# Maximum pass of an attention kernel: items of 64 queries of two heads in place of 128 queries of one head

## The chip, the cores and the metric

The kernel runs on one core of one Trainium2 chip. The metric is the device time of one execution in microseconds. A core has TensorE (matmuls; in the rows PE, its weight loads PEld), VectorE (DVE), ScalarE (ACT), GpSimd (POOL) and SyncE (SP), which issues most of the DMAs. Each works through its own queue in order and waits on semaphores.

## The reference

One transformer layer in float32, batch 4, sequence 1024, width 128:

```python
Q, K, V = (proj(W_Q), proj(W_K), proj(W_V))          # 16 heads of 8
Q = _apply_rope(Q, cos, sin)
K = _apply_rope(K, cos, sin)
scores = jnp.einsum('bhsd,bhtd->bhst', Q, K) / jnp.sqrt(jnp.float32(D_K))
scores = jnp.where(causal[None, None], scores, -jnp.inf)
attn = jax.nn.softmax(scores, axis=-1)
out = jnp.einsum('bhst,bhtd->bhsd', attn, V)
...
x = _layernorm(x + attention(x) @ W_O.T)
x = _layernorm(x + experts(x))    # 8 experts of 128-512-128 with gelu, top 2 by a softmax gate
```

## The kernel before

The program has three stages. Up to some 46 us it projects Q, K and V, applies the rotation and splits Q and K into three bf16 parts each, which go out to DRAM as stacks and come back as operands of 56 rows a head pair. Then comes attention, interleaved with the output projection, the layer norm, the gate and the routing of the batch before. From some 590 us on the experts run over 72 gathered tiles, and the second norm ends it.

Attention is worked off in 16 units, one for each batch (4) and group of four heads (4). In a unit the four heads sit in two halves of the partitions (parity `par`: rows 0 to 63 and 64 to 127) and two slots. A unit has two passes.

- The maximum pass ("A" items, `pass_a_items`) computes scores with the queries on the partitions of PSUM and the keys along the row, and reduces them to the maximum of each query. An item is one bank of the three-bank ring: 128 queries of one head (or of both slots, where at most 256 keys are needed) by up to 512 keys. 40 items make a unit. Where the item holds the diagonal, two mask products go first (L703 over the last 128 keys, L705 over the last 64): a half identity `half_sb` times `mask_sb` puts -1e30 where a key lies behind the query. Then L708 adds the scores: 64 rows of the array, 128 columns, so form 64*128. VectorE reads the bank with one `tensor_reduce` (L1157) into `mx`.
- The exponential pass has 12 steps. Each computes scores with the keys on the partitions ("QK", L734, two halves of the partitions into two banks, once for each slot), ScalarE takes the exponential (L867), GpSimd blanks the diagonal (L1408), and "PV" (L754, four heads in four column strips of 32, fp32) accumulates the output and the sum of the weights.

The maxima get into the second pass as three more rows of the operand: GpSimd splits `mx` into three bf16 parts (`SPLIT`, L1379 to L1385), TensorE turns them (`MT`, L716), VectorE copies the 48 rows into `mparts` (L1164), and SyncE writes them into `qst` (`MROWS`, L571). The outputs are turned by `OT` (L763) and scaled.

The order is written out by `schedule()`: while unit u goes through its exponential steps, the A items of unit u+1 are dealt out over these steps, in proportion to the steps' columns (`a_quota`). Each step stands as QK of slot 0, half of the items, QK of slot 1, the other items, PV of the step before. In the eight-bank PSUM three banks are the ring, four take the scores of the second pass and one the output. TensorE may fill a ring bank once VectorE has read what stood in it three entries earlier:

```python
if r is not None and r >= RING:
    pe.wait_ge(ring_read, at(r - RING + 1, RING_BATCH))
```

Unit 0 has its maximum pass ahead of everything. The middle batches are a hardware loop of two turns. The maximum pass of the kernel before, on TensorE:

```python
mm(view[:, :, n - P:n], half_sb[rows, 0, :], mask_sb[rows, 0, 0:k, :], ...)
mm(view[:, :, n - P // 2:n], half_sb[rows, 1, :], mask_sb[rows, 1, 0:k, P // 2:P], ...)
for m, slot_ in enumerate(slots):
    last = mm(ring[:, bank, m * n:(m + 1) * n], qst[rows, ...], kst[rows, v % NG, slot_, t0:t0 + n], ...)
```

Of the kernel before, what the change touches and what calls it, by code (L numbers as in the profile page):

```python
# [21 lines left out]
BF16 = mybir.dt.bfloat16  # L22
# [4 lines left out]
P = 128  # L27
B, S, D = 4, 1024, 128
# [10 lines left out]
MROW = 32  # L39

# [24 lines left out]
def pass_a_items():  # L65

    items = []
    for sb in range(BT):
        whole, rest = divmod((sb + 1) * P, CH)
        parts = [(CH * i, CH) for i in range(whole)] + ([(CH * whole, rest)] if rest else [])  # L70
        for t0, n in parts:
            masked = t0 + n == (sb + 1) * P
            if 2 * n <= CH:
                items += [(par, sb, t0, n, (0, 1), masked) for par in (0, 1)]
            else:
                items += [(par, sb, t0, n, (slot,), masked) for slot in (0, 1) for par in (0, 1)]
    return items
# [17 lines left out]
HALF_ROWS = GH * 3 * BT // 2  # L95

A_HALF = sum(1 for it in A_ITEMS if it[1] < CH // P)
# [174 lines left out]
def build(nc, xT, x, w, wg, bg, w1, w2,  # L272
          cs, ident, halves, maskA, before, tile128, tokens, tiles, first_row, out):
    ctx = ExitStack()
    with ctx:
        def sb(name, shape, dt=F32):
            return ctx.enter_context(nc.sbuf_tensor(name, shape, dt))

        def sem(name):
            return ctx.enter_context(nc.semaphore(name))  # L280
# [19 lines left out]
        half_f = sb("half_f", [P, 2, P])  # L300
        half_sb = sb("half_sb", [P, 2, P], BF16)
        mask_f = sb("mask_f", [P, 2, P])
        mask_sb = sb("mask_sb", [P, 2, 2, P], BF16)
# [47 lines left out]
        mx = sb("mx", [P, 2, GH, BT])  # L351
        mx2 = sb("mx2", [P, 2, GH, BT // 2])
        mrem = sb("mrem", [P, 2, GH, BT])
        zero = sb("zero", [P, GH, BT])

        msp_all = sb("msp", [P, 5 * HALF_ROWS], BF16)
        msp = msp_all[:, 0:4 * HALF_ROWS].rearrange("p (u c a j s n) -> p u c a j s n", u=2, c=2, a=2, j=3, s=2)
# [73 lines left out]
        mask_turns = sem("mask_turns")  # L431
        dve = sem("dve")
# [37 lines left out]
        def _(sp):  # L470
# [20 lines left out]
            sp.dma_start(half_f[:, :, :], halves).then_inc(loads, 16)  # L491
            sp.dma_start(mask_f[:, :, :], maskA).then_inc(loads, 16)
# [55 lines left out]
            def visit(e, r, at):  # L548
# [17 lines left out]
                elif e[0] == "MROWS":  # L566
# [82 lines left out]
        def _(pe):  # L649
# [34 lines left out]
            def visit(e, r, at):  # L684
# [7 lines left out]
                if kind == "A":  # L692
# [3 lines left out]
                    par, sb_, t0, n, slots, is_masked = A_ITEMS[i]  # L696
                    rows = slice(64 * par, 64 * par + 64)
                    k = len(slots)
                    if is_masked:
# [218 lines left out]
        def _(ve):  # L918
# [11 lines left out]
            for c in range(NCH):  # L930
# [10 lines left out]
                if c >= 2:  # L941
# [7 lines left out]
            v.tensor_copy(half_sb[:, :, :], half_f[:, :, :]).then_inc(masks_ready, 1)  # L949
            v.tensor_copy(mask_sb[:, :, :, :], mask_f[:, :, :].unsqueeze(2).broadcast_to([P, 2, 2, P])  # L950
                          ).then_inc(masks_ready, 1)
# [190 lines left out]
            def visit(e, r, at):  # L1142
# [8 lines left out]
                if kind == "A":  # L1151
                    unit, i = e[1:]
                    par, sb_, t0, n, slots, is_masked = A_ITEMS[i]
                    hs = slice(2 * slots[0] + par, 2 * slots[-1] + par + 1, 2)
                    dst = mx[:, unit % 2, hs, sb_] if t0 == 0 else mx2[:, unit % 2, hs, sb_ - BT // 2]
                    src = ring[:, bank, 0:len(slots) * n].rearrange("p (k n) -> p k n", k=len(slots))
                    read(v.tensor_reduce(dst, src, AX.X, ALU.max, negate=True))  # L1157
                    if i == NA - 1:

                        ve.wait_ge(ring_read, at(r + 1, RING_BATCH))  # L1160
                        v.tensor_tensor(mx[:, unit % 2, :, BT // 2:BT], mx[:, unit % 2, :, BT // 2:BT],
                                        mx2[:, unit % 2, :, :], ALU.min).then_inc(mx_ready, 1)
# [158 lines left out]
        def _(pool):  # L1321
# [32 lines left out]
            def visit(e, r, at):  # L1354
# [11 lines left out]
                elif e[0] == "SPLIT":  # L1366
# [9 lines left out]
                    none = by_parity(zero[:, :, :])  # L1376
                    part = [msp[:, unit % 2, c, :, j, :, :] for j in range(3)]
# [136 lines left out]
```

## Time and profile before

| | us |
|---|---|
| median of 3 runs | 820.85 |
| lowest and highest | 820.37, 832.62 |
| profiled execution | 823.58 |
| its span, first to last instruction | 821.8 |
| of it up to the first A item | 46.6 |
| attention, 46.6 to 590 | 543.4 |
| experts and output | 231.8 |

The profile is of one execution. Its page lists busy time by engine and groups of instructions by line; the trace behind it can be asked for stretches of time, waits and the chain of work that ended last. A matmul's end is modelled, and matmuls overlap in the pipeline of the array: the start of the next one says more than the length of one.

### The profile page before, as it was taken

The numbers are of one execution on the slowest core, as the hardware profiler recorded it, in microseconds if no ns is written. First come the engines' busy times: TensorE is split into PE (matmuls) and PEld (weight loads), VectorE is DVE, ScalarE is ACT, GpSimd is POOL, SyncE is SP. The second block draws the span as 40 slices with busy tenths as digits, with TensorE's granted clock in tenths as the row PEclk, the third lists the DMA queues.
The fourth block names the chain that finished last, engine by engine and source line by source line (L and its number), as shares of the span: only waits on it lengthen the run. The fifth ranks groups of instructions, "written<-read, shape, count | busy, mean of one in ns | idle before, by whom it ended". The sixth has DMA issues, their size and how long they took to land.

```text
span 821.8 us, 18980 instructions
## 1 busy us (share of the span) xinstructions
PE 683.3 (83%) x5560; PEld 362.6 (44%) x5561; DVE 584.6 (71%) x1467; ACT 443.5 (54%) x840; POOL 320.7 (39%) x577
## 2 busy tenths in 40 slices
PE   7987999999898868989889998988789857899830
PEld 3432333334343222434323333332278857798830
DVE  7886888888979867798988888896436712222266
ACT  2532676666455554556557655556647524466524
POOL 5961223322213265221328512226614555344551
PEclk9975999999879988998989998899989968899985
DMA  8893255011010120101012011000186745687923
GB/s 274 267 343 125 72 132 162 8 46 48 1 48 6 49 74 22 48 1 48 7 47 80 25 38 46 1 3 22 34 211 200 209 122 147 174 225 210 300 85 114
DMA packets 67352, 83.70 MB, mean 102 GB/s; under 512 B 9266, under 2 KB 46776, under 8 KB 67264
## 3 DMA queue, kind: packets, MB, share of 16 engines
q1 hardware_dynamic: 62912, 74.04, 30.5%
q0 software_dynamic: 4352, 8.53, 3.0%
q8 instruction: 49, 0.80, 0.4%
q14 instruction: 39, 0.32, 0.1%
HBM read 55.77 MB, written 26.90 MB: 101 GB/s over the span
## 4 chain that ended last, share of the span: by engine, by line
PE 50%; DVE 22%; issue 9%; ACT 5%; DMA 4%; SPq 4%; another core or an unknown queue 3%; POOL 2%; DVEq 0%; ACTq 0%; POOLq 0%
PE banks L754 14%; DVE mx L1157 14%; PE banks L708 9%; PE banks L823 6%; PE banks L734 5%; PE banks L812 5%; PE banks L703 2%; PE banks L763 2%; ACT region L867 2%; PE banks L655 2%; DMA region<-pairs 1%; ACT x_sb L910 1%; PE banks L832 1%; SPq L597 1%
## 5 line engine op out<-in xcount | busy, mean ns | idle before, releaser
L1157 DVE TENSOR_REDUCE mx<-banks 128x1 f32<-128x512 f32 (+3 forms) x640 | 366.0, 630 | 46.9 <-PE banks L708 41.5
L867 ACT ACTIVATE region<-banks 128x1024 f32<-128x1024 f32 (+3 forms) x256 | 201.3, 840 | 169.4 <-PE banks L734 159.7
L708 PE MATMUL banks<-region 64*128 64x512 bf16 (+3 forms) x768 | 196.0, 352 | 17.2 <-DVE mx L1157 15.1
L734 PE MATMUL banks<-region 64*128 64x512 bf16 (+3 forms) x768 | 141.6, 347 | 20.7 <-ACT region L867 11.4
L754 PE MATMUL banks<-region 128*32 128x512 f32 (+3 forms) x1024 | 123.1, 555 | 0.9 <-POOL region L1408 0.8
L867 ACT ACTIVATE cs_sb<-banks 128x1024 f32<-128x1024 f32 (+2 forms) x128 | 91.2, 759 | 42.4 <-PE banks L734 41.8
L1418 POOL DMA_INDIRECT results<-region,dest x72 | 71.7, 996 | 105.1 <-DVE region L1285 71.9
L703 PE MATMUL banks<-mask_sb,half_sb 64*128 64x128 bf16 (+1 forms) x384 | 84.7, 252 | 22.6 <-DVE mx L1157 17.3
L1279 DVE TENSOR_TENSOR region<-banks,w1e 128x128 f32<-128x128 f32 x72 | 21.0, 291 | 110.8 <-PE banks L812 66.3
L823 PE MATMUL banks<-region,w1e 128*128 128x128 f32 x576 | 83.2, 291 | 19.3 <-ACT region L893 13.9
L1408 POOL TENSOR_SCALAR_AFFINE_SELECT region<-region 128x256 f32<-128x256 f32 x160 | 64.2, 410 | 87.7 <-ACT region L867 85.1
L734 PEld LDWEIGHTS banks<-region 64*128 64x128 bf16 x768 | 42.4, 95 | 122.9 <-issue 47.3
L1408 POOL TENSOR_SCALAR_AFFINE_SELECT cs_sb<-cs_sb 128x256 f32<-128x256 f32 x96 | 38.6, 412 | 143.4 <-ACT cs_sb L867 142.6
L708 PEld LDWEIGHTS banks<-region 64*128 64x128 bf16 x768 | 65.2, 100 | 56.0 <-DVE mx L1157 42.9
L812 PE MATMUL banks<-w_sb,region 128*128 x576 | 83.3, 290 | 3.9 <-issue 1.8
L823 PEld LDWEIGHTS banks<-region,w1e 128*128 128x128 f32 x576 | 75.9, 205 | 21.4 <-ACT region L893 15.6
L901 ACT ACTIVATE region<-banks,w1e 128x128 f32<-128x128 f32 x288 | 82.9, 379 | 0.5 <-PE banks L823 0.5
L812 PEld LDWEIGHTS banks<-w_sb,region 128*128 128x128 f32 x576 | 74.3, 200 | 8.1 <-issue 6.7
L1394 POOL DMA_INDIRECT pairs<-xT_sb,slot x64 | 63.0, 985 | 36.9 <-issue 21.8
L705 PE MATMUL banks<-mask_sb,half_sb 64*128 64x64 bf16 (+1 forms) x384 | 71.3, 209 | 0.0
L893 ACT COPY region<-banks 128x128 f32<-128x128 f32 x72 | 19.2, 267 | 93.1 <-PE banks L832 67.5
L703 PEld LDWEIGHTS banks<-mask_sb,half_sb 64*128 64x128 bf16 x384 | 35.2, 97 | 61.9 <-DVE mx L1157 46.4
(177 smaller groups left out, 687.8 us busy)
## 6 DMA issues: line engine op xcount, KB each, us to landing
w1e<-in_w SPq DMA_DIRECT2D x72, 322.0 KB
region<-stack_q SPq DMA_DIRECT2D x64, 112.0 KB
region<-stack_k SPq DMA_DIRECT2D x32, 224.0 KB
region<-pairs SPq DMA_DIRECT2D x72, 66.0 KB
region<-results SPq DMA_DIRECT2D x8, 512.0 KB, 4.9
stack_q<-x_sb SPq DMA_DIRECT2D x8, 384.0 KB, 3.6
stack_k<-x_sb SPq DMA_DIRECT2D x8, 384.0 KB, 4.5
stack_q<-x_sb SPq DMA_DIRECT2D x8, 256.0 KB, 3.9
```

The lines of the kernel that those rows point to most:

```text
L703: mm(view[:, :, n - P:n], half_sb[rows, 0, :], mask_sb[rows, 0, 0:k, :], start=True, stop=False, skip_group_check=True)
L705: mm(view[:, :, n - P // 2:n], half_sb[rows, 1, :], mask_sb[rows, 1, 0:k, P // 2:P], start=False, stop=False, skip_group_check=True)
L708: last = mm(ring[:, bank, m * n:(m + 1) * n], qst[rows, v % NG, sb_ // 4, slot_, sb_ % 4 * P:(sb_ % 4 + 1) * P], kst[rows, v % NG, slot_, ...
L734: last = mm(score[:, slot_, par, 0:n], kst[rows, u % NG, slot_, j * P:(j + 1) * P], qst[rows, u % NG, c, slot_, s0 - c * CH:s0 - c * CH + ...
L754: last = mm(pv[32 * h:32 * h + 32, s0 - c * CH:s0 - c * CH + n], vx[:, u % NG, j, h, :], probs[(2 * e[1] + slot_) % 6][:, par, 0:n], start ...
L812: last = mm(down[k % 2], hg[:, k % 2, hc * P:(hc + 1) * P], w2_sb[:, bass.ds(e, 1), hc, :].rearrange("p a n -> p (a n)"), start=(hc == 0), ...
L823: last = mm(hidden[k % 2][:, hc * P:(hc + 1) * P], w1e[:, k, hc * P:(hc + 1) * P], xgT[:, k % 2, :], start=(hc == 0), stop=(hc == HC - 1), ...
L867: nc.scalar.activation(probs[i % 6][:, :, 0:n], score[:, i % 2, :, 0:n], ACT.Exp, scale=SCALE).then_inc(exp_done, 1)
L901: nc.scalar.activation(hg[:, k % 2, cols], hidden[k % 2][:, cols], ACT.Gelu_apprx_tanh, bias=w1e[:, k, HID + hc:HID + hc + 1]).then_inc(ge ...
L1157: read(v.tensor_reduce(dst, src, AX.X, ALU.max, negate=True))
L1408: pp.affine_select(out=block_, in_=block_, compare_op=ALU.is_ge, fill=0.0, base=0, pattern=[[0, 2], [1, P]], channel_multiplier=-1).then_i ...
L1418: pp.indirect_dma_start(out=results, out_offset=bass.IndirectOffsetOnAxis(ap=dest[:, k, :], axis=0), in_=ys[:, k, :], in_offset=None, boun ...
```

## The change

An A item becomes 64 queries of two heads, one in each half of the partitions: the head of rows 0 to 63 writes partitions 0 to 63 of the bank, that of rows 64 to 127 the other 64. The queries are cut into 16 pieces of 64, and an item reaches to the end of its piece's keys, (piece + 1) * 64 in place of (sb + 1) * 128. Again 40 items make a unit, 24 with a mask, with 17,408 columns for VectorE in place of 18,432. The mask is one product of 64 rows by 128 columns over the last 64 keys (two identities side by side) in place of two. Each slot of an item has two matmuls with a tile position, 64 rows by 64 columns each. An item without a mask increments a semaphore of its own. `mx`, the split, `mparts` and the DMAs follow: the maxima are `[slot, piece]` with the head pair along the partitions.

The diff, cut to what computes:

```diff
@@ pass_a_items
-    for sb in range(BT):
-        whole, rest = divmod((sb + 1) * P, CH)
+    for piece in range(S // QP):
+        whole, rest = divmod((piece + 1) * QP, CH)
         parts = [(CH * i, CH) for i in range(whole)] + ([(CH * whole, rest)] if rest else [])
         for t0, n in parts:
-            masked = t0 + n == (sb + 1) * P
+            masked = t0 + n == (piece + 1) * QP
             if 2 * n <= CH:
-                items += [(par, sb, t0, n, (0, 1), masked) for par in (0, 1)]
+                items.append((piece, t0, n, (0, 1), masked))
             else:
-                items += [(par, sb, t0, n, (slot,), masked) for slot in (0, 1) for par in (0, 1)]
+                items += [(piece, t0, n, (slot,), masked) for slot in (0, 1)]
...
-HALF_ROWS = GH * 3 * BT // 2
+HALF_ROWS = 3 * PIECES
...
@@ SyncE, MROWS
                     for par in (0, 1):
                         sp.dma_start(qst[64 * par + MROW:64 * par + MROW + 3, v % NG, c, :, :],
-                                     mparts[par * 3 * BT:(par + 1) * 3 * BT, v % 2, c, :]
+                                     mparts[:, v % 2, c, QP * par:QP * (par + 1)]
                                      ).then_inc(mrows[c][v % 2], 16)
@@ TensorE, A
                     if is_masked:
                         view = ring[:, bank, 0:k * n].rearrange("p (k n) -> p k n", k=k)
-                        mm(view[:, :, n - P:n], half_sb[rows, 0, :], mask_sb[rows, 0, 0:k, :], start=True, stop=False,
+                        mm(view[:, :, n - QP:n], half_sb[0:QP, :], mask_sb[0:QP, 0:k, :], start=True, stop=False,
                            skip_group_check=True)
-                        mm(view[:, :, n - P // 2:n], half_sb[rows, 1, :], mask_sb[rows, 1, 0:k, P // 2:P],
-                           start=False, stop=False, skip_group_check=True)
+                    else:
+                        pe.sem_inc(item_turns, 1)
                     for m, slot_ in enumerate(slots):
-                        last = mm(ring[:, bank, m * n:(m + 1) * n], qst[rows, v % NG, sb_ // 4, slot_, sb_ % 4 * P:(sb_ % 4 + 1) * P],
-                                  kst[rows, v % NG, slot_, t0:t0 + n], start=(m == 0 and not is_masked),
-                                  stop=(m == k - 1), skip_group_check=True)
+                        for rows in heads:
+                            last = mm(ring[rows, bank, m * n:(m + 1) * n],
+                                      qst[rows, v % NG, piece * QP // CH, slot_, at_:at_ + QP],
+                                      kst[rows, v % NG, slot_, t0:t0 + n], start=(m == 0 and not is_masked),
+                                      stop=(m == k - 1), tile_position=(rows.start, rows.start), skip_group_check=True)
                     last.then_inc(ring_full, 1)
@@ VectorE, A
-                    hs = slice(2 * slots[0] + par, 2 * slots[-1] + par + 1, 2)
-                    dst = mx[:, unit % 2, hs, sb_] if t0 == 0 else mx2[:, unit % 2, hs, sb_ - BT // 2]
+                    mine = slice(slots[0], slots[-1] + 1)
+                    dst = mx[:, unit % 2, mine, piece] if t0 == 0 else mx2[:, unit % 2, mine, piece - PIECES // 2]
@@ GpSimd, SPLIT
-                    cols = slice(c * BT // 2, (c + 1) * BT // 2)
-                    by_parity = lambda a: a[:, :, cols].rearrange("p (s a) n -> p a s n", a=2)
-                    neg, rest = by_parity(mx[:, unit % 2, :, :]), by_parity(mrem[:, unit % 2, :, :])
+                    cols = slice(c * PIECES // 2, (c + 1) * PIECES // 2)
+                    neg, rest = mx[:, unit % 2, :, cols], mrem[:, unit % 2, :, cols]
```

Two places of TensorE's queue, as they stand in the program. In the changed kernel L707 is the mask product, L713 the scores, L740 QK, L760 PV (before: L703 and L705, L708, L734, L754). In a row the shape is the output's, so `128x384` is 384 keys for 128 columns of the array, `64x384` for 64.

TensorE, unit 0, third step of the exponential pass, with masked items of unit 1; before:

```order
L703 MATMUL banks<-mask_sb,half_sb 128x128 [waits ring_read]
L705 MATMUL banks<-mask_sb,half_sb 128x64
L708 MATMUL banks<-region 128x384
L734 MATMUL banks<-region 128x256 [waits exp_done]
L734 MATMUL banks<-region 128x256
L703 MATMUL banks<-mask_sb,half_sb 128x128 [waits ring_read]
L705 MATMUL banks<-mask_sb,half_sb 128x64
L708 MATMUL banks<-region 128x384
L703 MATMUL banks<-mask_sb,half_sb 128x128 [waits ring_read]
L705 MATMUL banks<-mask_sb,half_sb 128x64
L708 MATMUL banks<-region 128x384
L754 MATMUL banks<-region 32x512 [waits masked,vx_ready,v_read]
```

And the same step now:

```order
L707 MATMUL banks<-mask_sb,half_sb 128x64 [waits ring_read]
L713 MATMUL banks<-region 64x320 x2
L740 MATMUL banks<-region 128x256 [waits exp_done]
L740 MATMUL banks<-region 128x256
L707 MATMUL banks<-mask_sb,half_sb 128x64 [waits ring_read]
L713 MATMUL banks<-region 64x320 x2
L707 MATMUL banks<-mask_sb,half_sb 128x64 [waits ring_read]
L713 MATMUL banks<-region 64x384 x2
L760 MATMUL banks<-region 32x512 [waits masked,vx_ready,v_read]
```

Before, all rows but the last have 128 columns of the array; now the scores have 64, between masks and QK that have 128, so the number changes five times ahead of L760 where it didn't change at all.

TensorE, unit 0, a later step, with items that have no mask; before:

```order
L734 MATMUL banks<-region 128x512 [waits exp_done]
L734 MATMUL banks<-region 128x512
L703 MATMUL banks<-mask_sb,half_sb 128x128 [waits ring_read]
L705 MATMUL banks<-mask_sb,half_sb 128x64
L708 MATMUL banks<-region 128x512
L708 MATMUL banks<-region 128x512 [waits ring_read]
L734 MATMUL banks<-region 128x512 [waits exp_done]
L734 MATMUL banks<-region 128x512
L708 MATMUL banks<-region 128x512 [waits ring_read] x2
L754 MATMUL banks<-region 32x128 [waits masked]
```

And now:

```order
L740 MATMUL banks<-region 128x512 [waits exp_done]
L740 MATMUL banks<-region 128x512
L707 MATMUL banks<-mask_sb,half_sb 128x64 [waits ring_read]
L713 MATMUL banks<-region 64x512 x2
L713 MATMUL banks<-region 64x512 [waits ring_read]
L713 MATMUL banks<-region 64x512
L740 MATMUL banks<-region 128x512 [waits exp_done]
L740 MATMUL banks<-region 128x512
L713 MATMUL banks<-region 64x512 [waits ring_read]
L713 MATMUL banks<-region 64x512
L707 MATMUL banks<-mask_sb,half_sb 128x128 [waits ring_read]
L713 MATMUL banks<-region 64x64 x4
```

Each L713 of 512 keys has a partner for the other head behind the same wait, and the last item of the step is now a short masked one of 64 keys. Around the QK pair in the middle the number of columns changes from 64 to 128 and back.

## Rows read from the trace of the kernel before

**Rows 1.** The page: span, and busy time of each engine.

```profile
span 821.8 us, 18980 instructions
PE 683.3 (83%) x5560; PEld 362.6 (44%) x5561; DVE 584.6 (71%) x1467; ACT 443.5 (54%) x840; POOL 320.7 (39%) x577
```

**Rows 2.** Windows by stage: length; busy us PE, PEld, DVE, ACT, POOL; clock; DMA share, GB/s.

```profile
46.60:73.50 26.90, 20.48 (x97) 7.44 (x97) 22.45 (x42) 5.24 (x7) 12.59 (x14) 0.57 0.85 288
...
85.24:196.20 110.96, 103.02 (x1002) 39.22 (x1003) 97.52 (x189) 75.56 (x105) 33.65 (x100) 1.00 0.27 77
196.20:569.00 372.80, 326.88 (x2812) 131.25 (x2808) 316.78 (x753) 210.93 (x286) 125.61 (x300) 0.92 0.11 33
...
590.00:821.80 231.80, 165.76 (x1312) 156.37 (x1308) 94.56 (x406) 110.93 (x394) 100.15 (x98) 0.86 0.63 177
```

**Rows 3.** Windows of two neighbouring units, same columns.

```profile
112.97:140.71 27.74, 25.66 (x250) 9.68 (x250) 24.35 (x48) 18.91 (x27) 8.41 (x25) 1.00 0.69 187
140.71:168.44 27.73, 25.66 (x250) 9.67 (x250) 24.34 (x48) 18.90 (x27) 8.41 (x25) 1.00 0.11 35
```

**Rows 4.** Chain of work, 140.70 to 168.44 us, then (second row) 300 to 420 us.

```profile
by line: PE banks L754 29.3%; DVE mx L1157 22.2%; PE banks L708 16.0%; PE banks L734 10.2%; issue 7.8%; ACT region L867 6.0%; PE banks L763 4.3%; PE banks L703 2.5%; PE banks L716 1.5%; DVE attn L1172 1.0%; DVE rden L1170 1.0%; PE banks L70
...
140.71 3.08 DVE mx L1157 x5
...
by line: DVE mx L1157 20.3%; PE banks L754 17.6%; PE banks L708 13.2%; issue 12.4%; PE banks L734 7.5%; another core or an unknown queue 5.8%; PE banks L703 3.5%; PE banks L763 2.5%; PE banks L792 1.6%; PE banks L770 1.5%; PE banks L705 1.0
```

**Rows 5.** Timeline of TensorE, 91.5 to 94.6 us: start, duration, form rows*columns.

```profile
91.59 0.28 PE L703 MATMUL banks<-mask_sb,half_sb 64*128 64x256 bf16 x1 [0.19 <-DVE mx L1157]
91.71 0.22 PE L705 MATMUL banks<-mask_sb,half_sb 64*128 64x128 bf16 x1
91.77 0.38 PE L708 MATMUL banks<-region 64*128 64x256 bf16 x2
92.07 1.07 PE L754 MATMUL banks<-cs_sb,region 128*32 128x512 f32 x8
93.07 0.66 PE L763 MATMUL banks<-id_sb,ot 128*128 128x128 f32 x4
93.66 0.39 PE L734 MATMUL banks<-region 64*128 64x512 bf16 x2
93.89 0.38 PE L708 MATMUL banks<-region 64*128 64x512 bf16 x2
94.10 0.38 PE L734 MATMUL banks<-region 64*128 64x512 bf16 x2
94.40 0.39 PE L708 MATMUL banks<-region 64*128 64x512 bf16 x1
```

**Rows 6.** Groups by shape: busy us, mean ns of one.

```profile
L1157 DVE TENSOR_REDUCE mx<-banks 128x1 f32<-128x512 f32 x384 | 243.6, 683 | 24.9 <-PE banks L708 22.0 <-issue 0.6
...
L708 PEld LDWEIGHTS banks<-region 64*128 64x128 bf16 x768 | 65.2, 100 | 56.0 <-DVE mx L1157 42.9 <-DVE attn L1172 5.0 <-DVE y L1222 1.8
L1157 DVE TENSOR_REDUCE mx<-banks 128x1 f32<-128x384 f32 x128 | 63.8, 550 | 10.2 <-PE banks L708 8.6 <-issue 0.7
```

**Rows 7.** Who waited for whom, 140.7 to 168.44 us: us, times, longest.

```profile
DVE mx L1157 <- PE banks L708: 3.3, 10, 0.6
...
PEld banks L708 <- DVE mx L1157: 1.9, 5, 0.6
...
PEld banks L703 <- DVE mx L1157: 1.6, 4, 0.5
```

**Rows 8.** L731 on TensorE's sequencer: ns min/median/max.

```profile
L731 PEldq EVENT_SEMAPHORE  x15: 51/51/51, 82.1 to 574.5; - x15
```

**Rows 9.** Chain before the first QK; who waited for the DMA of L571 (us, times).

```profile
66.90 6.60 DMA region<-mparts
...
  PE banks L734: 3.9, 1
```

**Rows 10.** L1379 on GpSimd, by shape.

```profile
L1379 POOL TENSOR_TENSOR msp<-mx,zero 128x16 bf16<-128x16 f32 x32 | 7.1, 222 | 80.2 <-DVE mx L1157 62.4 <-DVE mx L1161 17.8
```

More of the change, by code:

```diff
@@ L39 @@
 MROW = 32
+QP = 64
+PIECES = S // QP
 Q_PLACES = ((0, (0, 3, 6)), (1, (1, 2)), (2, (5,)))
@@ L94 @@
 C_LAST = [max(k for k, st in enumerate(B_STEPS) if st[0] == c) for c in range(2)]
-HALF_ROWS = GH * 3 * BT // 2
-A_HALF = sum(1 for it in A_ITEMS if it[1] < CH // P)
+HALF_ROWS = 3 * PIECES
+A_HALF = sum(1 for it in A_ITEMS if it[0] < PIECES // 2)
 def diagonal(k):
@@ L299, in build @@
         idb_sb = sb("idb_sb", [P, P], BF16)
[L300 to L303, printed above, removed]
+        half_f = sb("half_f", [P, P])
+        half_sb = sb("half_sb", [P, P], BF16)
+        mask_f = sb("mask_f", [P, QP])
+        mask_sb = sb("mask_sb", [P, 2, QP], BF16)
         fill = sb("fill", [P, 2, S], BF16)
@@ L350, in build @@
         rden = sb("rden", [P, 2, 4 * GH])
[L351 to L354, printed above, removed]
+        mx = sb("mx", [P, 2, 2, PIECES])
+        mx2 = sb("mx2", [P, 2, 2, PIECES // 2])
+        mrem = sb("mrem", [P, 2, 2, PIECES])
+        zero = sb("zero", [P, 2, PIECES])
         msp_all = sb("msp", [P, 5 * HALF_ROWS], BF16)
-        msp = msp_all[:, 0:4 * HALF_ROWS].rearrange("p (u c a j s n) -> p u c a j s n", u=2, c=2, a=2, j=3, s=2)
+        msp = msp_all[:, 0:4 * HALF_ROWS].rearrange("p (u c j s n) -> p u c j s n", u=2, c=2, j=3, s=2)
         mparts = sb("mparts", [HALF_ROWS, 2, 2, P], BF16)
@@ L431, in build @@
         mask_turns = sem("mask_turns")
+        item_turns = sem("item_turns")
         dve = sem("dve")
@@ L490, in _ @@
             sp.dma_start(id_sb[:, :], ident).then_inc(loads, 16)
-            sp.dma_start(half_f[:, :, :], halves).then_inc(loads, 16)
-            sp.dma_start(mask_f[:, :, :], maskA).then_inc(loads, 16)
+            sp.dma_start(half_f[:, :], halves).then_inc(loads, 16)
+            sp.dma_start(mask_f[:, :], maskA).then_inc(loads, 16)
             sp.dma_start(wg_sb[:, :], wg).then_inc(loads, 16)
@@ L1160, in visit @@
                         ve.wait_ge(ring_read, at(r + 1, RING_BATCH))
-                        v.tensor_tensor(mx[:, unit % 2, :, BT // 2:BT], mx[:, unit % 2, :, BT // 2:BT],
+                        upper = slice(PIECES // 2, PIECES)
+                        v.tensor_tensor(mx[:, unit % 2, :, upper], mx[:, unit % 2, :, upper],
                                         mx2[:, unit % 2, :, :], ALU.min).then_inc(mx_ready, 1)
@@ L1372, in visit @@
                         pool.wait_ge(mx_ready, at(unit + 1, NG))
-                    cols = slice(c * BT // 2, (c + 1) * BT // 2)
-                    by_parity = lambda a: a[:, :, cols].rearrange("p (s a) n -> p a s n", a=2)
-                    neg, rest = by_parity(mx[:, unit % 2, :, :]), by_parity(mrem[:, unit % 2, :, :])
-                    none = by_parity(zero[:, :, :])
-                    part = [msp[:, unit % 2, c, :, j, :, :] for j in range(3)]
+                    cols = slice(c * PIECES // 2, (c + 1) * PIECES // 2)
+                    neg, rest = mx[:, unit % 2, :, cols], mrem[:, unit % 2, :, cols]
+                    none = zero[:, :, cols]
+                    part = [msp[:, unit % 2, c, j, :, :] for j in range(3)]
                     done = 8 * unit + 4 * c
@@ L1484 @@
     q, k = np.arange(P)[:, None], np.arange(P)[None, :]
-    row = np.arange(P)[:, None, None] % 64 + 64 * np.arange(2)[None, :, None]
-    col = np.arange(P)[None, None, :]
-    halves = np.where(col == row, np.float32(1.0), np.float32(0.0))
+    row = np.arange(P)[:, None] % QP
+    col = np.arange(QP)[None, :]
+    halves = np.tile(np.where(col == row, np.float32(1.0), np.float32(0.0)), (1, 2))
     mask_a = np.where(col > row, np.float32(-1e30), np.float32(0.0))
```

12 lines of the change are left out of this document (6 added, 6 removed).

## The prediction

> **What bounds the kernel now.** I read the page first, then the windows by stage, then one unit of the attention stage in full. The page gives a span of 821.8 us with TensorE busy 83% and VectorE 71% [rows 1]; these are means over unlike stages, so they settle nothing. The profiled execution took 823.58 us, 2.73 us above the median of the runs (820.85); I work against 823.58 and take 2.7 off at the end. The change touches the maximum pass alone, which lives between 46.6 and 569 us; what stands behind 590 us (231.8 us of experts and output) stays [rows 2]. In the four units from 85.24 to 196.20 us nothing else is interleaved and the clock is 1.00: 27.74 us a unit. The eleven units whose maxima are taken after that have the routing work of an earlier batch beside them: 372.8 us for what is 11 to 12 units, some 31.5 us each, at a mean clock of 0.92 [rows 2].
>
> One unit is so regular that two neighbours agree to 0.01 us: VectorE 24.35 us busy, TensorE 25.66 of 27.74 [rows 3]. Both engines look near full, so the chain decides: of such a unit it spends 22.2% on the maxima of L1157 and more than 60% on TensorE lines (L754 29.3%, L708 16.0%, L734 10.2%, L763 4.3%, L703 2.5%); in a later batch it is 20.3% against some 48%, with 12.4% "issue" [rows 4]. The reader should see an engine pair that takes turns: VectorE rules in runs of consecutive items (five in 3.08 us), TensorE everywhere else.
>
> How full TensorE is by columns: a column takes 1/2.4 ns at the full clock, an fp32 column two. A unit's maximum pass streams 18,432 columns of scores (7.68 us) and 6,144 of masks (2.56), QK 4,608 per slot in pairs (3.84), PV 4,608 x 4 (7.68), the transposes 0.96: 22.7 us. Laying the unit's 250 matmuls [rows 3] side by side by start and columns, 20.6 us are covered; 2.1 us fall together, because matmuls on the two halves of the partitions run at once: two 512-column ones stand in 0.39 us where one alone takes 0.39 too [rows 5].
>
> **The price of another tile shape.** The form names rows*columns of the array. Within 64*128 a matmul follows its predecessor when its columns are through: 256 columns 0.107 us, L703 to L705 0.12; 512 columns 0.213 us, L708 to L734 0.21. Where the shape changes there is more. L708 starts at 91.77 with 2 x 256 columns (0.213), so it is through at 91.98, and L754 (128*32) starts at 92.07: 0.09. From L763 (128*128) to L734 four fp32 transposes need 0.43, and 0.59 pass: at most 0.16. From L754 (128*32) to L763 (128*128), where the number of rows stays and only the columns change, 1.00 us pass for 0.85 of columns: at most 0.15 [rows 5]. I take 0.10 us a change, the clean end of 0.09 to 0.16.
> The Trainium skill, "TensorEngine Tiling (Array Packing)", Key Properties, says that changing the tiling mode, not just the tile, drains the engine, and its list of modes has 64x64 and 64x128 as separate ones. The rows agree for the shapes that occur; the pair 64*128 and 64*64 occurs in none of them.
>
> **The change, part by part.**
> *VectorE.* Still 40 items a unit, but 17,408 columns for 18,432. The maxima cost 683 ns at 512 columns and 550 at 384: 1.04 ns a column [rows 6]. So 1,024 x 1.04 = 1.06 us less a unit, 17 us in all, of which only what lies on the chain counts: 0.2 of it, 0.2 us a unit, about 3.5 us.
> *TensorE, columns.* Scores: 17,408 columns, each streamed for two heads on different quarters of the array, 7.25 us if the two run together. Masks: 24 products of 64 columns a slot, 2,048 columns, 0.85 us for 2.56. Sum with the rest 20.6 us. That is what was covered before: the 2.1 us saved are the 2.1 us that used to fall together, since an item of 64*64 can't share time with a QK of 64*128 if a change lies between.
> *TensorE, shapes.* This is the cost. Mask products stay 64*128 (64 rows, 128 columns), the scores become 64*64, QK stays 64*128. Counting through the order of a batch gives 116 changes before and 324 after: 208 more, 52 a unit (mask to scores 24, scores to the next mask 9, scores to QK 11, QK to unmasked scores 8). 52 x 0.10 = 5.2 us a unit. In unit 0, whose pass runs alone, some 46 more.
> *What hides it.* TensorE's waits. A unit of 27.74 us holds 20.6 of columns, 28 changes (2.8) and about 0.9 of small gaps, so 3.4 us of waits. They are for VectorE above all: the loads of L708 and L703 alone stand 1.9 and 1.6 us behind L1157 (loads run ahead, so not all of this is idle array); VectorE in turn waits 3.3 us for L708 [rows 7]. Afterwards columns, 80 changes and small gaps make 29.5 us: even with no wait left the unit is 1.8 us longer. With all waits kept it is 5.2 longer. The waits sit in the runs that VectorE rules, and there the changes are free; I take a third hidden: 3.5 us a unit, for four units 13.9. In the later units, 31.5 us long with 5 us and more of such waits, I take half: 2.6 us, for eleven units 28.6. Unit 0, where the chain is mostly L1157: a third of 4.6, 1.5.
> *Semaphores on TensorE.* Each of 16 unmasked items a unit increments item_turns. Such an instruction takes 51 ns in the sequencer [rows 8]; between nothing and 16 x 0.051 = 0.8 us a unit. The sequencer runs ahead of the array, and the only time it binds is after a wait; nothing taken.
> *Second loads.* Weights of 64x64 twice per slot in place of one of 64x128. A load of L708 takes 100 ns [rows 6] and lies under columns that flow, as before. Only where an item has under 128 columns a slot can it stick out: between nothing and 4 x 0.10 us a unit; nothing taken.
> *Maxima to rows.* The copy keeps 48 partitions; each DMA into qst reads 48 pieces of 128 bytes for 24 of 256. It is on the path once, 6.60 us before the first QK, and later nobody waits for it but 3.9 us at one place [rows 9]. Twice the pieces may cost 0 to 2 us there; I take 0.3. The four POOL steps keep their 16 elements, 222 ns [rows 10]; nothing.
> Sum: 13.9 + 28.6 + 1.5 + 0.3 - 3.5 = +40.8 us. 823.6 + 40.8 - 2.7 = 861.7.
>
> **Rivals.**
> *The change of shape is free between 64*128 and 64*64.* For it: the rows stay 64, no row of before shows the pair, and within a shape the gap is nil [rows 5]. Against: L754 to L763 keeps its rows as well, and pays. Then TensorE's columns are level, VectorE saves between 3.5 (its share of the chain) and 17 us; half-way, 823.6 - 10 - 2.7 = 811. It decides in favour of the change once a change costs under 0.01 us.
> *The two heads' products don't run together.* They write one bank, halves of the partitions, from different rows of the array. Row pairs that run together now (L734, L708) write different banks [rows 5]. What speaks against it: the four heads of L754 write one bank from four column strips, 8 passes of 512 fp32 columns in 1.07 us, so a bank takes several writers. If they ran one after the other: 7.25 us a unit more, 15 units 109 us, no waits left to hide anything: 861.7 + 109 = 971.
> The Trainium skill, same page, Gotcha 1 (PSUM Pressure), says that different row tiles can't access the same PSUM bank at the same time. No run here shows it; it would give the 971.
> *Waits swallow the changes.* TensorE gives up all its waits for VectorE and nothing shifts: 1.8 us a unit for four units, nothing for the eleven, VectorE's 3.5 off: 823.6 + 7.2 - 3.5 - 2.7 = 825. For it: VectorE keeps 0.84 of its engine. Against: the waits are where VectorE rules, the changes are everywhere.
>
> **Numbers.** Forecast 0.68, at 862, own range 838 to 904 (upper end: 5.2 us exposed in each of 15 units and 4.6 in unit 0). Waits swallow it 0.10 (825), free change 0.14 (811), products in turn 0.08 (971). A difference of 2%, 16.4 us, is about what a measurement of this kernel can tell from no change. Slower by over 2% (above 837): 0.68 + 0.08 and a little of the third, 0.77. Within 2%: 0.19. Faster: a quarter of the free-change case, 0.04. Range 830 to 904, which leaves out most of 0.14 and 0.08 and small tails. The granted clock is a bounded unknown in it: 0.92 over the later units could move by 0.03, some 10 us either way.
>
> **What would show it.** In the unit without routing work: about 31.2 us for 27.74; scores of 64*64 starting some 0.10 us after the mask's columns are through, and QK 0.10 after the scores'; 128 columns' worth of masks for 384; two heads' matmuls 4 ns apart, "x2" in 0.39 us. VectorE's L1157 349 us for 366, its idle time before it up, TensorE's share of the chain up. A gap under 0.02 us at mask to scores means the first rival; a pair of 512 columns in 0.6 us the second; a unit of 29.5 us the third.

## The result, and the profile after

The changed kernel takes 847.22 us (median of 4 runs, 844.91 to 848.06) against 823.13 for the kernel before in the same series: a ratio of 1.0263, 95% interval 1.0221 to 1.0305. It is slower, as forecast. 862 was forecast, so the loss is 24 us in place of 41.

The page of the changed kernel, its span, busy times, the small packets and the two groups of the maximum pass:

```profile
span 846.3 us, 20004 instructions
...
PE 739.6 (87%) x5944; PEld 367.6 (43%) x5945; DVE 574.5 (68%) x1467; ACT 447.7 (53%) x840; POOL 320.8 (38%) x577
...
DMA packets 68891, 83.58 MB, mean 99 GB/s; under 512 B 10930, under 2 KB 48312, under 8 KB 68800
...
L1162 DVE TENSOR_REDUCE mx<-banks 128x1 f32<-128x512 f32 (+7 forms) x640 | 354.6, 604 | 79.6 <-PE banks L713 72.5
...
L713 PE MATMUL banks<-region 64*64 64x512 bf16 (+7 forms) x1536 | 232.2, 344 | 9.6 <-DVE mx L1162 9.1
```

The maxima on the page of the kernel before:

```profile
L1157 DVE TENSOR_REDUCE mx<-banks 128x1 f32<-128x512 f32 (+3 forms) x640 | 366.0, 630 | 46.9 <-PE banks L708 41.5
```

VectorE is 10.1 us less busy than before [rows 1] and TensorE 56.3 more. The idle time ahead of the maxima went from 46.9 to 79.6 us, nearly all of it spent waiting for the scores (L713): VectorE's smaller work went into waiting.

Windows of the changed kernel, each from one unit's first output to another's (length; busy us PE, PEld, DVE, ACT, POOL; clock). The first holds three units without routing work, the second the eleven units after unit 4, the third unit 11 alone (units are counted from 0), the last what follows the start of the last output:

```profile
97.65:191.85 94.20, 92.90 (x824) 32.03 (x822) 71.61 (x141) 58.03 (x78) 25.43 (x75) 1.00 0.29 79
225.31:610.58 385.27, 361.63 (x3085) 131.52 (x3083) 308.48 (x770) 219.48 (x295) 136.73 (x315) 0.97 0.10 32
477.44:510.89 33.45, 32.99 (x292) 12.48 (x291) 25.88 (x50) 19.52 (x26) 11.35 (x28) 1.00 0.11 36
621.20:846.30 225.10, 162.99 (x1276) 154.91 (x1276) 95.86 (x406) 109.39 (x390) 97.22 (x92) 0.86 0.65 182
```

The same stretches of the kernel before, the first three:

```profile
93.76:176.96 83.20, 76.98 (x752) 29.02 (x752) 73.02 (x141) 56.70 (x78) 25.24 (x75) 1.00 0.32 90
206.93:586.16 379.23, 330.15 (x2837) 130.44 (x2835) 317.19 (x770) 217.84 (x296) 137.41 (x315) 0.91 0.10 32
454.27:484.29 30.02, 27.92 (x268) 11.60 (x267) 26.25 (x50) 19.10 (x26) 11.35 (x28) 1.00 0.12 40
```

The last stretch stayed as it was: 225.1 us, for 225.4 before (596.4 to 821.8). A unit without routing work went from 27.73 (83.20 / 3) to 31.40 us (94.20 / 3), 3.67 more. The eleven later ones went from 379.2 to 385.3 together, 0.55 more each, while their mean clock rose from 0.91 to 0.97. From the first output of unit 0 to that of unit 4 it is 14.5 us (127.66 for 113.17), for the eleven units 6.0, and unit 0's first output comes 3.9 later (97.65 for 93.76): together 24.4, against 24.5 by the spans.

Timeline of TensorE in the changed kernel, same columns as [rows 5] (a row merges neighbouring instructions of one line):

```profile
97.55 0.39 PE L740 MATMUL banks<-region 64*128 64x512 bf16 x2
97.87 0.62 PE L713 MATMUL banks<-region 64*64 64x512 bf16 x4
98.42 0.39 PE L740 MATMUL banks<-region 64*128 64x512 bf16 x2
98.64 0.19 PE L707 MATMUL banks<-mask_sb,half_sb 64*128 64x64 bf16 x1
98.76 0.32 PE L713 MATMUL banks<-region 64*64 64x320 bf16 x2
99.06 0.20 PE L707 MATMUL banks<-mask_sb,half_sb 64*128 64x64 bf16 x1
99.19 0.32 PE L713 MATMUL banks<-region 64*64 64x320 bf16 x2
99.44 1.06 PE L760 MATMUL banks<-region 128*32 128x512 f32 x8
```

Take columns from starts. QK (L740, 512 columns, 0.213) starts at 97.55 and the scores (L713, 64*64) at 97.87: 0.32 us, so 0.11 for the change. From QK to a mask (98.42 to 98.64, both 64*128) it is 0.22, so nothing. From a mask of 64 columns (0.027) to the scores 0.12: 0.09. Those changes between 64*128 and 64*64 cost what the other changes cost before. From scores of 320 columns (0.133) to the next mask it is 0.30: besides a change of 0.10 some 0.07 are left that these rows don't explain. The four L713 of 97.87, two items, stand in 0.62 us where one 512-column matmul takes 0.39: two items in sequence are 0.39 + 0.213 = 0.60, so the two heads of an item run together, in one bank.

The chain of the changed kernel, 140.70 to 168.44 us, to be held against the first row of [rows 4]:

```profile
by line: PE banks L713 32.9%; PE banks L760 29.4%; PE banks L740 17.5%; DVE mx L1162 9.4%; PE banks L707 5.7%; PE banks L769 4.2%; PE banks L722 1.3%; issue 1.2%
```

The maxima went from 22.2% of the chain to 9.4%, and TensorE's lines from 64% to 91%. A unit of the changed kernel is longer than this window; over a whole one (129.05 to 160.45 us) the maxima are 8.3%. TensorE has become the bound of a unit.

### The profile page after: what moved, and what is told of

It reads as the page before. It is cut to its first block, busy times and chain, and to the rows that moved or that the text cites. A ratio compares the mean times of both kernels' runs of the same rounds, so it can differ in the third digit from the quotient of the medians.

```text
span 846.3 us, 20004 instructions
## 1 busy us (share of the span) xinstructions
PE 739.6 (87%) x5944; PEld 367.6 (43%) x5945; DVE 574.5 (68%) x1467; ACT 447.7 (53%) x840; POOL 320.8 (38%) x577
## 2 busy tenths in 40 slices
DMA packets 68891, 83.58 MB, mean 99 GB/s; under 512 B 10930, under 2 KB 48312, under 8 KB 68800
## 4 chain that ended last, share of the span: by engine, by line
PE 60%; DVE 16%; issue 7%; SPq 5%; DMA 3%; another core or an unknown queue 3%; ACT 3%; POOL 1%; DVEq 0%; ACTq 0%; POOLq 0%
PE banks L713 17%; PE banks L760 16%; PE banks L740 9%; DVE mx L1162 8%; PE banks L818 4%; PE banks L829 4%; PE banks L707 3%; PE banks L769 2%; SPq L601 1%; DMA region<-pairs 1%; SPq L602 1%; ACT x_sb L916 1%; SPq L595 1%; PE banks L659 1%
## 5 line engine op out<-in xcount | busy, mean ns | idle before, releaser
L1162 DVE TENSOR_REDUCE mx<-banks 128x1 f32<-128x512 f32 (+7 forms) x640 | 354.6, 604 | 79.6 <-PE banks L713 72.5
L873 ACT ACTIVATE region<-banks 128x1024 f32<-128x1024 f32 (+3 forms) x256 | 204.6, 839 | 175.3 <-PE banks L740 169.2
L713 PE MATMUL banks<-region 64*64 64x512 bf16 (+7 forms) x1536 | 232.2, 344 | 9.6 <-DVE mx L1162 9.1
L740 PE MATMUL banks<-region 64*128 64x512 bf16 (+3 forms) x768 | 127.4, 338 | 11.0 <-DMA region<-mparts 4.3
L760 PE MATMUL banks<-region 128*32 128x512 f32 (+3 forms) x1024 | 117.5, 532 | 0.9 <-POOL region L1413 0.8
L713 PEld LDWEIGHTS banks<-region 64*64 64x64 bf16 x1536 | 71.0, 106 | 96.5 <-issue 74.4
L740 PEld LDWEIGHTS banks<-region 64*128 64x128 bf16 x768 | 35.5, 93 | 147.2 <-issue 93.1
L707 PE MATMUL banks<-mask_sb,half_sb 64*128 64x64 bf16 (+1 forms) x384 | 79.6, 207 | 14.5 <-DVE mx L1162 10.9
L829 PEld LDWEIGHTS banks<-region,w1e 128*128 128x128 f32 x576 | 75.7, 205 | 22.2 <-ACT region L899 19.0
L707 PEld LDWEIGHTS banks<-mask_sb,half_sb 64*128 64x128 bf16 x384 | 36.5, 95 | 50.2 <-DVE mx L1162 32.5
L760 PE MATMUL banks<-cs_sb,region 128*32 128x512 f32 (+2 forms) x512 | 51.4, 474 | 1.3 <-POOL cs_sb L1413 1.3
```

The lines of the kernel that those rows point to most:

```text
L707: mm(view[:, :, n - QP:n], half_sb[0:QP, :], mask_sb[0:QP, 0:k, :], start=True, stop=False, skip_group_check=True)
L713: last = mm(ring[rows, bank, m * n:(m + 1) * n], qst[rows, v % NG, piece * QP // CH, slot_, at_:at_ + QP], kst[rows, v % NG, slot_, t0:t0 ...
L740: last = mm(score[:, slot_, par, 0:n], kst[rows, u % NG, slot_, j * P:(j + 1) * P], qst[rows, u % NG, c, slot_, s0 - c * CH:s0 - c * CH + ...
L760: last = mm(pv[32 * h:32 * h + 32, s0 - c * CH:s0 - c * CH + n], vx[:, u % NG, j, h, :], probs[(2 * e[1] + slot_) % 6][:, par, 0:n], start ...
L829: last = mm(hidden[k % 2][:, hc * P:(hc + 1) * P], w1e[:, k, hc * P:(hc + 1) * P], xgT[:, k % 2, :], start=(hc == 0), stop=(hc == HC - 1), ...
L873: nc.scalar.activation(probs[i % 6][:, :, 0:n], score[:, i % 2, :, 0:n], ACT.Exp, scale=SCALE).then_inc(exp_done, 1)
```

## The experiments

Changes of tile shape a unit, counted in the program's order: 29 in the kernel before, 81 in the changed one.

**Masks in the scores' shape.** In the changed kernel:

```diff
-                        mm(view[:, :, n - QP:n], half_sb[0:QP, :], mask_sb[0:QP, 0:k, :], ...)
+                        pe.sem_inc(item_turns, 1)
+                        for rows in heads:
+                            mm(view[rows, :, n - QP:n], half_sb[rows, 0:QP], mask_sb[rows, 0:k, :], ...,
+                               tile_position=(rows.start, rows.start), ...)
```

> Edit: in the changed kernel each mask product is two of 64x64 (one for each half of the partitions) in place of one of 64x128, so that masks and scores of an item have one shape and only QK, PV and the transposes differ. Changes of tile shape go from 81 to 63 a unit. Theory (each change costs some 0.10 us, of which some 0.07 reaches the time, since 52 more changes made the unit without routing work 3.66 us longer): unit 31.40 - 18 x 0.07 = 30.1 us, whole run about 830 to 835 us. Rival (what costs is that an item now has two heads' matmuls with loads of their own, or that neighbouring items no longer share time, whatever the shapes): unit stays at 31.4 us or grows, since a mask now takes two matmuls, whole run 847 us or more.

Measured: 833.04 us, ratio to the kernel before 1.0109 (1.0059 to 1.0160). Three units without routing work, then units 4 to 15:

```profile
94.64:186.09 91.45, 89.08 (x896) 31.82 (x894) 71.33 (x141) 58.07 (x78) 25.39 (x75) 1.00 0.29 83
218.71:595.52 376.81, 345.30 (x3329) 129.84 (x3331) 307.35 (x770) 219.06 (x296) 137.05 (x315) 0.98 0.11 33
```

A unit takes 30.48 us (91.45 / 3), 0.92 less than 31.40 although it has 24 matmuls and 24 increments more. That is less than the 1.3 expected; the 24 increments, at the 12 ns each of a run further down, are 0.3 of it. Of the whole run's loss over half is gone (1.0109 for 1.0263) with 18 of the 52 added changes. The eleven later units take 376.81 us, less than the 379.23 of the kernel before, at a clock of 0.98 for 0.91.

**All three in one shape.** As the run before, and:

```diff
+                    pe.sem_inc(item_turns, 1)
                     for par in (0, 1):
                         rows = slice(64 * par, 64 * par + 64)
-                        last = mm(score[:, slot_, par, 0:n], kst[rows, u % NG, slot_, j * P:(j + 1) * P],
-                                  qst[rows, ...], start=True, stop=True)
+                        for kh in (0, 64):
+                            last = mm(score[kh:kh + 64, slot_, par, 0:n],
+                                      kst[rows, u % NG, slot_, j * P + kh:j * P + kh + 64],
+                                      qst[rows, ...], start=True, stop=True, tile_position=(64 * par, kh))
```

> Edit: as the run before, and QK too as four products of 64x64 (two halves of the rows by two halves of the keys). Changes of shape are back at 29 a unit as in the kernel before, while VectorE keeps its 1,024 columns less. Theory: the unit without routing work is at or just under 27.74 us (27.2 to 27.9), the run 810 to 825 us, equal to the kernel before or faster. Rival (two heads' matmuls and their loads cost by themselves): unit over 30 us, run over 840 us.

Measured: 818.87 us, ratio 0.9942 (0.9910 to 0.9974). It beats the changed kernel clearly and the kernel before by 0.6%.

```profile
92.91:179.78 86.87, 80.51 (x1042) 34.92 (x1044) 70.70 (x141) 56.70 (x78) 25.10 (x75) 1.00 0.31 87
211.24:578.37 367.13, 318.75 (x3865) 141.19 (x3863) 307.48 (x771) 216.15 (x296) 136.58 (x315) 0.99 0.11 34
```

The rival falls: with two heads' matmuls and all their loads kept, and QK doubled on top, a unit is 28.96 us, 2.44 less than in the changed kernel. But it isn't at 27.74 or under, as expected: 1.2 us remain over the kernel before with the same number of changes. So the 0.6% by which the whole run is faster don't come from the units without routing work. They come from the eleven later ones, 367.13 us for 379.23, where the mean clock is 0.99 for 0.91. In unit 11, the one of the eleven with a clock of 1.00 in both, this kernel is slower too (30.74 us for 30.02). The timeline of this run shows shapes that share time again:

```profile
92.81 0.41 PE L744 MATMUL banks<-region 64*64 64x512 bf16 x4
93.05 0.38 PE L715 MATMUL banks<-region 64*64 64x512 bf16 x1
93.05 0.38 PE L744 MATMUL banks<-region 64*64 64x512 bf16 x2
93.06 0.59 PE L715 MATMUL banks<-region 64*64 64x512 bf16 x3
```

The four products of a QK (first row) stand in 0.41 us, where two of 64*128 took 0.39. Scores of an item (L715) and the next QK (L744) start within 0.01 us of each other. Once their shapes agree they overlap again, so the 1.2 us are hardly time that is no longer shared.

**The kernel before with QK alone in 64x64.** Only the edit of QK above.

> Edit: the kernel before, with QK alone as four products of 64x64; items, masks and VectorE untouched. Changes of shape go from 29 to 63 a unit. Theory: unit 27.74 + 34 x 0.07 = 30.1 us, up to 31 where QK no longer shares time with an item's scores; whole run 838 to 855 us. Rival (the shape is free, the cost sits in the new items): unit 27.7 us, run 821 us.

Measured: 848.99 us, ratio 1.0286 (1.0226 to 1.0346).

```profile
95.89:186.09 90.20, 89.21 (x898) 32.42 (x896) 74.32 (x142) 57.68 (x78) 25.55 (x75) 1.00 0.30 83
218.28:610.28 392.00, 364.12 (x3369) 137.71 (x3367) 319.10 (x770) 220.51 (x296) 137.69 (x315) 0.93 0.10 31
```

30.07 us a unit, as expected. The old items with the new QK lose as much of the whole run as the new items with the old QK; together they lose nothing. At the full clock, in the unit without routing work, the old items with the new QK cost 2.34 us, the new items with the old QK 3.67, and both together 1.23. So neither shape is slow. What costs is the boundary: the change itself, 0.09 to 0.11 us in the timeline, and the time that products on both sides of it no longer share. How a unit's loss divides between the two, these runs don't show.

**More increments.** Two more on TensorE's queue ahead of the scores of each item.

> Edit: the changed kernel with two more semaphore increments on TensorE's queue ahead of the scores of every item (80 a unit more). Theory (the sequencer runs ahead of the array, increments are free): unit 31.4 us, run 847 us within 0.5%. Rival (each takes its 51 ns out of the array's time): 80 x 0.051 = 4.1 us a unit, unit 35.5 us, run about 905 us, and then the changed kernel's own 16 increments cost 0.8 us a unit.

Measured: 859.68 us, ratio 1.0437 (1.0364 to 1.0509).

```profile
97.97:195.12 97.15, 93.97 (x824) 32.55 (x822) 72.00 (x141) 58.31 (x78) 25.55 (x75) 1.00 0.28 77
```

Neither (two runs): a unit takes 32.38 us, 0.98 more for 80 increments, 12 ns each. They aren't free and don't cost their 51 ns. The changed kernel's 16 are worth 0.2 us a unit.

**The kernel before with more columns.** The scores of the 16 unmasked items are issued twice:

```diff
+                    if not is_masked:
+                        mm(ring[:, bank, 0:n], qst[rows, ...], kst[rows, v % NG, slots[0], t0:t0 + n],
+                           start=True, stop=False, skip_group_check=True)
                     for m, slot_ in enumerate(slots):
```

> Edit: the kernel before, with the scores product of each of the 16 unmasked items of a unit issued twice (512 columns each, 3.4 us of columns a unit at the full clock, the second starts the sum anew). No change of shape, nothing for VectorE. Theory of the clock (in the later units work on TensorE is paid back, since its idle times shrink and it is granted 2.4 GHz for more of the time): unit without routing work 29.5 to 31 us, mean clock between the first outputs of units 4 and 15 up from 0.91 to 0.95 or more, and these eleven units longer by under 1 us each. Rival (slack alone: the later units' waits hide work whatever the clock): clock stays at 0.91, and they are longer by 1 to 2 us each. Whole run 835 to 850 us.

Measured: 833.82 us, ratio 1.0113 (1.0070 to 1.0157).

```profile
95.39:183.41 88.02, 82.23 (x800) 31.48 (x799) 73.99 (x142) 56.84 (x78) 25.10 (x75) 1.00 0.30 85
214.79:593.96 379.17, 337.32 (x2997) 135.04 (x2995) 318.40 (x770) 217.25 (x296) 136.74 (x315) 0.95 0.10 32
```

A unit without routing work is 1.61 us longer (29.34), a little under the range given, and so is the whole run. The eleven later units take 379.17 us for 379.23: the same work, 1.6 us a unit where the clock is full, costs nothing in their sum, and the mean clock stands at 0.95 for 0.91. It isn't that they always have room for it. Unit 11, whose clock is 1.00 in both kernels, takes 31.35 us for 30.02, 1.33 more:

```profile
464.08:495.43 31.35, 29.56 (x284) 12.35 (x282) 26.57 (x51) 19.18 (x26) 11.27 (x28) 1.00 0.12 39
```

The rival (a constant clock, and 1 to 2 us a unit) falls.

**Keys rounded up to 128.** In the changed kernel the key range of a piece is `(piece // 2 + 1) * P` and the mask stays on its own 64 keys.

> Edit: the changed kernel, with the keys of an even piece rounded up to 128 again, so VectorE reads 18,432 columns a unit as in the kernel before, and each head pair's scores stream 1,024 columns more (0.43 us). The 64 keys behind an even piece's diagonal block have no mask, so the maximum is taken over 64 keys too many there. Theory (VectorE is a fifth of the chain, so its smaller work was worth 0.2 us a unit): unit 31.40 + 0.2 + 0.3 = 31.9 us, run 850 to 856 us. Rival (VectorE's saving counted in full and hid part of the loss): unit 31.40 + 1.06 + 0.3 = 32.8 us, run 865 us or more.

Measured: 852.66 us, ratio 1.0346 (1.0287 to 1.0405).

```profile
97.39:192.79 95.40, 94.01 (x824) 32.12 (x822) 74.61 (x141) 58.10 (x78) 25.57 (x75) 1.00 0.28 78
226.64:616.23 389.59, 364.12 (x3085) 131.04 (x3084) 318.12 (x770) 220.85 (x296) 137.95 (x315) 0.97 0.10 31
```

VectorE is 1.0 us a unit busier (74.61 for 71.61 over three units), and the unit 0.40 longer (31.80), which TensorE's 0.43 us of columns explain by themselves. In the changed kernel VectorE's saving was worth next to nothing.

**Both kernels again**, for second traces.

> The kernel before, unchanged, for a second trace. Units without routing work 27.7 us. Theory of the clock: the time of the later units follows their mean clock, so the same unit of the two traces differs by over 2 us where its clock differs by 0.1. Rival: a unit takes the same time in both, whatever its clock.

> The changed kernel, unchanged, for a second trace. Units without routing work 31.4 us. Theory: its mean clock over the eleven units from unit 4 to 15 is again 0.95 or more, above that of the kernel before run beside it by 0.03 or more. Rival: the first trace's 0.97 against 0.91 was chance.

Measured, one run each: 826.13 and 850.14 us. Of the kernel before, unit 4 in the first trace and in the second, unit 8 in the first and in the second, then units 4 to 15 of the second:

```profile
206.93:246.31 39.38, 35.20 (x284) 15.29 (x284) 33.63 (x88) 21.17 (x29) 8.59 (x25) 0.83 0.08 26
...
208.03:245.34 37.31, 32.77 (x284) 14.45 (x284) 33.65 (x88) 21.17 (x29) 8.59 (x25) 0.91 0.09 27
...
352.35:389.88 37.53, 32.79 (x284) 14.60 (x284) 33.64 (x89) 21.27 (x29) 8.58 (x25) 0.91 0.08 27
...
349.64:390.26 40.62, 36.18 (x284) 15.79 (x284) 33.88 (x89) 21.42 (x29) 8.63 (x25) 0.83 0.08 25
...
208.04:588.24 380.20, 332.41 (x2837) 131.21 (x2835) 317.58 (x771) 217.87 (x296) 137.57 (x315) 0.91 0.10 32
```

Of the changed kernel, unit 7 and units 4 to 15 of the second trace:

```profile
330.28:371.27 40.99, 38.24 (x292) 13.28 (x291) 26.30 (x50) 19.82 (x26) 11.59 (x28) 0.83 0.10 31
224.17:609.69 385.52, 362.62 (x3085) 131.13 (x3084) 308.86 (x770) 220.55 (x296) 137.57 (x315) 0.96 0.10 32
```

The difference of the clock is there again, 0.96 against 0.91, and so is that of time, 5.3 us. Unit 7 of the changed kernel takes 40.99 us at a clock of 0.83. In the first trace the same unit reads

```profile
332.40:368.07 35.67, 33.06 (x292) 12.57 (x291) 25.82 (x50) 19.52 (x26) 11.40 (x28) 1.00 0.12 35
```

35.67 at 1.00. Same program, same unit: 0.17 of clock are 5.3 us. In the kernel before, 0.08 of clock are 2.1 us in unit 4 and 3.1 in unit 8, as its expectation had it.

That gives a price. The clock has two levels, 1.2 and 2.4 GHz, so a mean of 0.83 over 40.99 us is 13.9 us at the lower one (2 x 0.17 x 40.99), and these cost 5.3: 0.38 us for each. The pairs of units 4 and 8 give 0.31 and 0.44 in the same way. It is under the 0.5 that would be lost if TensorE alone set the time.

**Fewer increments, and increments alone.** The all-64x64 kernel with its increments only inside the hardware loop, and the kernel before with one ahead of every item and every QK. At each of the three increments of the first (`at` gives a plain number only outside the loop):

```diff
-                    pe.sem_inc(item_turns, 1)
+                    if not isinstance(at(0, 1), int):
+                        pe.sem_inc(item_turns, 1)
```

> Edit: masks, scores and QK all as 64x64, with the increments ahead of them only inside the hardware loop (two turns of four units), none in the units before and after it. Theory (an increment costs 13 ns of a unit, since 80 more made it 1.0 us longer, and 64 of them explain most of the 1.2 us by which the all-64x64 unit stands above 27.73): units without routing work 28.1 us for 28.96, run 810 to 816 us, ratio to the kernel before 0.985 to 0.990. Rival (the 1.2 us are the score products of items and QK that no longer run at the same time): unit stays at 28.9 us, ratio 0.994.

> Edit: the kernel before, with one semaphore increment on TensorE's queue ahead of every item and every QK, 64 a unit, shapes untouched. Theory: 27.73 + 64 x 0.013 = 28.6 us for the unit without routing work, run 828 to 836 us. Rival (increments are free where no shape changes around them): unit 27.7 us, run 824 us.

Measured: 820.66 us, ratio 0.9913 (0.9879 to 0.9946), and 831.67 us, ratio 1.0077 (1.0045 to 1.0110). Three units without routing work of the first and of the second:

```profile
94.76:179.45 84.69, 79.62 (x1042) 32.61 (x1044) 70.39 (x141) 56.48 (x78) 25.24 (x75) 1.00 0.32 90
```

```profile
95.81:180.74 84.93, 78.25 (x752) 30.99 (x752) 73.05 (x141) 57.01 (x78) 25.11 (x75) 1.00 0.32 88
```

28.23 us for 28.96, and 28.31 for 27.73: 64 increments are worth 0.7 and 0.6 us, 9 to 11 ns each. They are more than half of what stood over after the all-64x64 run. The last 0.5 us (28.23 against 27.73) stays open, and is more than it looks, since VectorE and the masks have fewer columns than in the kernel before. The unit's chain in this run (122.99 to 151.22 us) has 18.7% for the maxima and 10.2% for ScalarE's L882, for 22.2% and 6.0% in [rows 4]: what VectorE gave up, 0.9 us, the exponentials took, 1.2. Why wasn't tried. The whole run missed the 810 to 816 us that were expected, and isn't told from the version with all increments, 0.9913 against 0.9942 with intervals that overlap; both are faster than the kernel before.

## Why the prediction was right, and where its size was off

*The price of a change of shape: right.* 0.10 us was taken, and the rows show 0.09 to 0.11 between 64*128 and 64*64. The rival "free" fell in the first trace, and the all-64x64 run shows it from the other side: 52 changes fewer, 2.44 us a unit less. The Trainium skill, "TensorEngine Tiling (Array Packing)", Key Properties, says that a change of tiling mode drains the engine; the trace agrees in that the next shape starts 0.09 to 0.11 us late.

*The unit without routing work: right.* +3.5 us was forecast, +3.67 measured, with a third of the changes hidden in waits. The chain's share of VectorE fell by more than half, as "TensorE gives up its waits" requires.

*Two heads in one bank: right.* Four matmuls of 512 columns in 0.62 us. The Trainium skill, same page, Gotcha 1, says that different row tiles can't access one bank at the same time; here two of them write the two halves of one bank's partitions at once, and the measurement decides.

*VectorE's saving: small, as taken, and smaller still.* 0.2 us a unit was taken; the run with rounded keys leaves about nothing beside TensorE's own columns. The prediction looked for 349 us of maxima; the page has 354.6. The saving in single durations is the 17 us that were reckoned (640 x 630 ns before, 640 x 604 after, 16.6 us), but busy time is less than such sums (366.0 us for 403.2, 354.6 for 386.6): the records overlap where reductions follow each other closely, and there is less of that after the change.

*Semaphores: off by their size only.* Nothing was taken of a range from 0 to 0.8 us a unit; 16 increments at 12 ns are 0.2 us, 3 us over the run. The reason given, that the sequencer binds only after a wait, isn't tested: the runs show what an increment costs, not where.

*The DMA of the maxima: as bounded.* 7.08 us on the chain (its row starts at 67.71 us) for 6.60 [rows 9], where 0.3 more was taken, and 1,664 more packets under 512 bytes (10,930 for 9,266). The unit-0 term as a whole came out larger than its 1.5 + 0.3: 3.9 us to the first output in this trace, but 1.6 between the two second traces (96.50 for 94.86), so it isn't settled to better than 2 us.

*The later units: the step that failed.* "I take half: 2.6 us, for eleven units 28.6." The measured sum is 6.0 us, 5.3 in the second pair of traces. The sum then gives 40.8 - 28.6 + 6.0 = 18 us; the rest up to 24 is the term of unit 0 (3.9 for 1.8), the first four units (14.5 for 13.9) and VectorE's 3.5, which the forecast took off apart while the measured times already hold whatever was saved. The prediction had named the clock as a bounded unknown, "some 10 us either way", and had it without a sign. It has a sign, and the run with more columns shows it with no change of shape at all: more work on TensorE, a clock of 0.95 for 0.91, and no time lost over the eleven units. How much of the gap it explains is an estimate from the rows. Before, 0.91 over 379.2 us is some 68 us at 1.2 GHz (2 x 0.09 x 379.2); after, 0.97 over 385.3 is some 23, and 0.96 over 385.5 in the second trace 31. So 37 to 45 us less stand at the lower level. At the 0.3 to 0.45 us each of the pairs above, that is an estimated 11 to 20 us given back, of the 22.6 by which the forecast was too high.

The rest is more hiding than the half that was taken. It shows where the clock is 1.00 in both kernels compared. In unit 5, with heavy routing work, the all-64x64 kernel and the changed one differ by 0.61 us:

```profile
247.11:281.27 34.16, 28.84 (x354) 12.12 (x355) 31.00 (x87) 19.13 (x26) 9.67 (x26) 1.00 0.10 30
```

```profile
264.31:299.08 34.77, 31.76 (x280) 11.26 (x278) 30.91 (x87) 19.38 (x26) 9.70 (x26) 1.00 0.10 30
```

In a unit without routing work the same 52 changes cost 2.44. VectorE is busy 31 of these 34 us. Unit 11, which the kernel before and the changed one both run at 1.00, hides hardly more than a unit without routing work: 30.02 us before and 33.45 after, +3.43. So one figure of 2.6 stood for units in which the changes cost from 0.6 to 3.4 us at the full clock, and for a clock that moved. What decides in each unit whether the clock falls was not tried.

## What to carry to other kernels

When products of different sizes alternate on TensorE, count the changes of rows*columns in the queue before counting columns: at 0.1 us each they were worth more here than 6% fewer columns for VectorE and two thirds of the mask columns. If one of several products that alternate gets a smaller shape, give it to all of them, even if it takes twice the instructions: neither the new items nor the new QK paid alone (1.026 and 1.029), together they were level with the kernel before or a little faster (0.994). That last gain isn't one of the shape: where the clock was full, a unit was still 1.2 us longer than before. And where the granted clock is under 1, work added to TensorE or taken from it comes back in part through the clock, so price it in a stretch with the clock at 1.00 and expect less elsewhere.

## What the runs showed of the hardware that I had not expected

- Two matmuls from different halves of the rows may write one bank at the same time if they write different halves of its partitions: 4 x 512 columns in 0.62 us.
- QK as four products of 64x64 streams in about the time of two of 64x128 (0.41 us for 0.39), and overlaps with scores of 64x64 in other banks: starts 0.01 us apart.
- An increment of a semaphore on TensorE's queue costs 9 to 12 ns of a unit where 51 ns stand in the sequencer's rows.
- 1.6 us of added columns a unit cost 1.3 to 1.6 us where the clock was 1.00, and nothing over eleven units where its mean had been 0.91, and left it at 0.95.
- One microsecond at 1.2 GHz in place of 2.4 cost 0.3 to 0.45 us in three pairs of the same unit.
